# Rebuilding the setup of a one-core attention and mixture-of-experts block

## What is computed

```python
mod = (silu(c) @ wmod).reshape(8, 6, 1, -1)            # sa, ca, ga, sb, cb, gb
h = layernorm(x) * (1 + ca) + sa
c_q = h @ w_dq.T                                       # 256 -> 192
q_c, q_r = c_q @ w_uq.T, c_q @ w_qr.T                  # content 16 x 16, rotary 16 x 64
c_kv = h @ w_dkv.T                                     # 256 -> 64, "latent"
k_c, v, k_r = c_kv @ w_uk.T, c_kv @ w_uv.T, h @ w_kr.T
q_r, k_r = rope(q_r, k_r)
x = x + ga * (softmax(mask(q @ k.T) * SCALE) @ v @ w_out.T)
h = layernorm(x) * (1 + cb) + sb
x = x + gb * experts(h)     # top-8 router over 32, 8 merged groups, silu(gate) * up, down
```

## Time and profile before

| what | value |
|---|---|
| time of the timed runs | 1141.07 us median of 3, 1139.87 to 1143.53 |
| time of the profiled execution | 1138.69 us |
| its span, first to last instruction | 1136.6 us |
| mean granted TensorE clock | 0.977 |
| PE busy | 1031.2 us, 91% |
| DVE busy | 754.6 us, 66% |
| ACT, POOL busy | 399.5 us and 419.9 us, 35% and 37% |
| first `score` matmul of batch 0 | 95.21 us from the start |

### The profile page before, as it was taken

One profiled execution on the slowest core, in us unless ns is written; L12 is line 12 of the kernel. 1 busy time (PEld: TensorE's weight loads), 2 busy tenths in 40 slices (PEclk: granted clock), 3 DMA queues, 4 the chain that ended last, 5 costly groups with the idle time before them and its releaser, 6 DMA issues.

```text
span 1136.6 us, 24953 instructions
## 1 busy us (share of the span) xinstructions
PE 1031.2 (91%) x9856; PEld 743.4 (65%) x9856; DVE 754.6 (66%) x1516; ACT 399.5 (35%) x715; POOL 419.9 (37%) x349
## 2 busy tenths in 40 slices
PE   7849999999999998999999998999999999999668
PEld 2636667766677666766677666776677666776456
DVE  3557858677676767668676777668586776766335
ACT  1432542145331642244422553225421543315310
POOL 1152643164342632244332633326431633426100
PEclk9978999999999999999999999999999999999979
DMA  6130000010002000020002000020001100010000
GB/s 193 28 103 2 2 2 1 25 43 2 1 1 67 2 2 1 2 66 2 2 1 66 2 2 1 1 67 1 2 1 37 31 2 1 1 48 2 2 0 19
DMA packets 22152, 23.59 MB, mean 21 GB/s; under 512 B 6298, under 2 KB 20058, under 8 KB 22050
## 3 DMA queue, kind: packets, MB, share of 16 engines
q1 hardware_dynamic: 22050, 22.02, 6.4%
HBM read 17.80 MB, written 4.21 MB: 19 GB/s over the span
## 4 chain that ended last, share of the span: by engine, by line
PE 82%; DVE 8%; issue 4%; ACT 4%; POOL 1%; DMA 1%; DVEq 0%; SPq 0%; POOLq 0%; ACTq 0%
PE ring L1083 16%; PE ring L947 12%; PE ring L948 10%; PE ring L949 10%; PE ring L1152 7%; PE av L1099 6%; PE ring L1063 6%; DVE mcol L829 3%; PE ring L1054 3%; PE ring L1071 1%; PE ring L1143 1%; PE ring L1007 1%; PE av L1112 1%; ACT pt L648 1%; ACT xn L607 1%
## 5 line engine op out<-in xcount | busy, mean ns | idle before, releaser
L648 ACT ACTIVATE pt<-ring 128x384 f32<-128x384 f32 (+1 forms) x384 | 171.0, 532 | 361.9 <-PE ring L1083 319.3
L829 DVE TENSOR_REDUCE mcol<-ring 128x1 f32<-128x128 f32 (+3 forms) x512 | 212.0, 483 | 51.8 <-PE ring L1063 49.7
L544 POOL TENSOR_SCALAR_AFFINE_SELECT pt<-pt 128x512 f32<-128x512 f32 x128 | 83.3, 663 | 350.3 <-ACT pt L648 350.3
L805 DVE TENSOR_TENSOR prod<-ring,table 128x1024 f32<-128x1024 f32 x128 | 156.1, 1222 | 78.4 <-PE ring L949 56.7
L1083 PE MATMUL ring<-rows 32*128 32x512 f32 (+3 forms) x3072 | 164.4, 327 | 20.5 <-DVE mcol L829 10.5
L535 POOL TENSOR_TENSOR rows<-prod,rows 128x1024 fp32r<-128x1024 f32 x64 | 152.4, 2385 | 82.5 <-ACT rows L628 82.5
L1083 PEld LDWEIGHTS ring<-rows 32*128 32x128 f32 x3072 | 119.3, 184 | 68.9 <-issue 35.3
L528 POOL TENSOR_TENSOR prod<-prod 128x512 f32<-128x512 f32 x64 | 84.7, 1323 | 134.2 <-DVE prod L805 133.9
L947 PE MATMUL ring<-h_hi,gu_lo 128*128 128x512 f32 x192 | 80.3, 418 | 14.2 <-DVE h_lo L790 14.2
L1099 PE MATMUL av<-pt,vals 128*17 128x512 f32 (+3 forms) x1024 | 83.4, 439 | 10.2 <-POOL pt L544 10.2
L947 PE MATMUL ring<-h_hi,wq_lo 128*128 128x512 f32 x192 | 83.8, 436 | 3.8 <-DVE cont L817 3.3
(11 more groups left out here) (157 smaller groups left out, 1650.8 us busy)
## 6 DMA issues: line engine op xcount, KB each, us to landing
xn<-x_dram SPq DMA_DIRECT2D x8, 512.0 KB, 4.1
xr<-x_dram SPq DMA_DIRECT2D x8, 512.0 KB, 3.8
out_dram<-xr SPq DMA_DIRECT2D x8, 512.0 KB, 3.1
gate_bc<-gates_scratch SPq DMA_DIRECT2D x8, 256.0 KB, 5.2
pt<-wmod_dram SPq DMA_DIRECT2D x1, 1536.0 KB, 9.0
pt<-gup_t_dram SPq DMA_DIRECT2D x16, 96.0 KB, 2.5
prod<-wu_t_dram SPq DMA_DIRECT2D x1, 640.0 KB, 5.0
xr<-wk_t_dram SPq DMA_DIRECT2D x1, 512.0 KB, 8.8
```

Source lines behind the costliest of these rows:

```text
L648: sc.activation(pt[:, PT_AT[n] + h * w:PT_AT[n] + (h + 1) * w], ps[:, 0:w], ACT.Exp, scale=SCALE).then_inc(exp_ready.sem, 1)
L805: ve.tensor_tensor(prod[:, s % PROD, :, :], ps[:, :].unsqueeze(1).broadcast_to([P, 2, S]), table[:, :, :], ALU.mult).then_inc(rotated.sem, 1)
L829: last = ve.reduce_max(mcol[:, q, h * HR + HD:h * HR + HD + 1], ps[:, at:at + (q + 1) * P], AX_X)
```

## The change

Only the setup is different; the list of the last batch is now written out (`LAST_ORDER`), and it has the same 185 steps in the same order as the filtered list had.

- The loads are issued in another order: the index list, `c` and `wmod` first, then `x`, the latent weights, the keys' weights, the weights for fusing, the small ones and the tables. `wu` and `w_dq` no longer go to `prod`: they go to `dn`, `room` and `wo`, so the loads of `wo` and of the down weights wait on SP for `fuse_read` of all six pieces. The 16 loads of gate and up weights stay behind `gates_read`.
- The order of the steps is new: `silu`, the layer norm, `mod`, the splits of the latent and key weights, `turn1`, `gates`, `modulate1`/`low1`, `fuse` 0, the split of the other small weights, `latent`. `fuse` 1 stands before the first `rope`, `fuse` 2 and 3 (the content columns) before group 1, `fuse` 4 and 5 (columns of groups 2 and 3) before `qcon.01`.
- `split_keys` is three steps with a count each. DVE's part of `gates` now stands ahead of `low1`.
- `kcon_hi`/`kcon_lo` stand ahead of `hi` of the same group, and `maxima`/`reduce` of group 0 between the steps of group 1. `shift.00` comes after `qcon.01`, and `spread` and both `split_ffn` are last.

```diff
-FUSE = [(c, at, min(512, NQ - at)) for c in range(EC) for at in range(0, NQ, 512)]
+FUSE = [(c, at, min(512, NQ - at)) for at in (0, NG * NROPE, 512) for c in range(EC)]
-latent.0 latent_hi.0 latent_lo.0 rope.0000 rotate.0000 rope.0001 rotate.0001 combine.000 kcon.00 hi.000 kcon_hi.00
-kcon_lo.00 lo.000 rope.0010 rotate.0010 rope.0011 rotate.0011 combine.001 qcon.00 hi.001 qcon_hi.00 qcon_lo.00
-lo.001 values.00 values_out.00 values.01 values_out.01 rope.0100 rotate.0100 rope.0101 rotate.0101 combine.010
-kcon.01 hi.010 kcon_hi.01 kcon_lo.01 lo.010 rope.0110 rotate.0110 rope.0111 rotate.0111 combine.011 qcon.01 hi.011
-qcon_hi.01 qcon_lo.01 lo.011
+latent.0 latent_hi.0 latent_lo.0 fuse.1 rope.0000 rotate.0000 rope.0001 rotate.0001 combine.000 kcon.00 kcon_hi.00
+kcon_lo.00 rope.0010 rotate.0010 rope.0011 rotate.0011 hi.000 lo.000 combine.001 fuse.2 fuse.3 hi.001 lo.001
+rope.0100 rotate.0100 qcon.00 qcon_hi.00 qcon_lo.00 rope.0101 rotate.0101 combine.010 values.00 values_out.00
+values.01 values_out.01 kcon.01 kcon_hi.01 kcon_lo.01 hi.010 maxima.000 reduce.000 lo.010 rope.0110 rotate.0110
+maxima.001 reduce.001 rope.0111 rotate.0111 combine.011 maxima.002 reduce.002 fuse.4 fuse.5 qcon.01 qcon_hi.01
+qcon_lo.01 shift.00 shifted.00 hi.011 lo.011 spread. split_ffn.0 split_ffn.1
...
-    out = [("stats1", 0), ("pow1", 0), ("fuse", 0), ("norm1", 0)] + [("fuse", i) for i in range(1, len(FUSE))]
-    out += [("silu",), ("mod",), ("split_keys",), ("turn1", 0, 0), ("turn1", 0, 1), ("modulate1", 0, 0), ("low1", 0, 0),
-            ("modulate1", 0, 1), ("low1", 0, 1), ("gates",)]
-    out += steps_of(SETUP_ORDER) + [("spread",)]
-    for i in range(NMAX):
-        out += [("maxima", 0, 0, i), ("reduce", 0, 0, i)]
-    return out + [("split_ffn", 0), ("shift", 0, 0), ("shifted", 0, 0), ("split_ffn", 1)]
+    out = [("silu",), ("stats1", 0), ("pow1", 0), ("norm1", 0), ("mod",), ("split_d",), ("split_k",), ("turn1", 0, 0), ("turn1", 0, 1),
+           ("gates",), ("modulate1", 0, 0), ("low1", 0, 0), ("modulate1", 0, 1), ("low1", 0, 1), ("fuse", 0), ("split_uv",)]
+    return out + steps_of(SETUP_ORDER)
...
+            chosen_at = [sp.value_load(idx_sb[0:1, g:g + 1], min_val=0, max_val=NX - 1) for g in range(G)]
             for g in range(G):
...
+            sp.wait_ge(fuse_read, len(FUSE))
+            sp.dma_start(wo[:, :, :], wo_p.rearrange("g p e -> p g e")).then_inc(ld_wo, 16)
+            for g in range(G):
                 for row, n in DOWN_PIECES[g]:
...
                     elif kind == "rope":
-                            pe.wait_ge(fuse_read, len(FUSE))
+                            pe.wait_ge(fuse_read, EC)
...
                     elif kind == "qcon":
+                        if part == "setup":
+                            pe.wait_ge(fuse_read, len(FUSE) if g else 2 * EC)
...
                     elif kind == "down":
+                        if isinstance(b, int) and b == 0 and i == 0:
+                            pe.wait_ge(ld_down, 16 * sum(map(len, DOWN_PIECES)))
```

More of the change, by code:

```diff
@@ L116, in body_steps @@
-def body_steps(last):
-    return [s for s in steps_of(BODY_ORDER) if s[1] == 0 or not last]
+LAST_ORDER = """
+loads.0 maxima.010 reduce.010 rope.0200 score.000 rotate.0200 exp.000 rope.0201 rotate.0201 maxima.011 rope.0210
+reduce.011 score.001 clear.000 combine.020 rotate.0210 rope.0211 exp.001 clear.001 maxima.012 value.000 rotate.0211
+value.001 reduce.012 score.002 shift.01 exp.002 combine.021 kcon.02 qcon.02 clear.002 kcon_hi.02 hi.020 shifted.01
+score.010 lo.020 qcon_hi.02 value.002 exp.010 hi.021 kcon_lo.02 clear.010 qcon_lo.02 attn_out.00 rope.0300 score.011
@@ new lines @@
+exp.011 lo.021 rope.0301 rotate.0300 maxima.020 value.010 rotate.0301 reduce.020 score.012 rope.0310 exp.012
+maxima.021 rotate.0310 reduce.021 combine.030 clear.011 clear.012 rope.0311 kcon.03 maxima.022 rotate.0311 qcon.03
+hi.030 value.011 kcon_hi.03 lo.030 qcon_hi.03 combine.031 hi.031 kcon_lo.03 reduce.022 value.012 qcon_lo.03 shift.02
+shifted.02 maxima.030 reduce.030 attn_out.01 score.020 exp.020 lo.031 score.021 exp.021 clear.020 maxima.031
+reduce.031 maxima.032 value.020 clear.021 reduce.032 value.021 score.022 shift.03 shifted.03 exp.022 clear.022
@@ new lines @@
+score.030 value.022 exp.030 attn_out.02 score.031 clear.030 exp.031 score.032 value.030 exp.032 clear.031 value.031
+clear.032 value.032 attn_out.03 mix.00 mix.01 mixed.00 mixed.01 stats2.0 pow2.0 norm2.0 turn2.00 turn2.01
+modulate2.00 modulate2.01 low2.00 low2.01 up.00 gate.00 logits.0 tanh.00 gated.00 gate.01 logits_out.0 gate.02
+tanh.01 top.0 gated.01 up.01 ex.0 tanh.02 upped.00 gate.03 gate.04 top2.0 turn_w.0 up.02 gated.02 tanh.03 wT.0
+gated.03 gate.05 upped.01 upped.02 tanh.04 tanh.05 gated.04 wT_lo.0 up.03 up.04 weigh.00 upped.03 weigh.01 weigh.02
@@ L236, in block_program @@
         av = ctx.enter_context(nc.psum_tensor("av", [P, 512], F32))
[L239 to L240 removed]
+        ld_wo, ld_d, ld_mod, ld_q, ld_k, ld_tab, ld_small, ld_ffn, ld_down, ld_idx = (
+            sem(n) for n in ("ld_wo", "ld_d", "ld_mod", "ld_q", "ld_k", "ld_tab", "ld_small", "ld_ffn", "ld_down", "ld_idx"))
         x_loaded = Count(sem("x_loaded"), 1, 16)
@@ L426, in x_rows @@
                 return x[bass.ds(b + ahead, 1), :, :].rearrange("o (t p) e -> p (o t) e", p=P)
+            sp.dma_start(idx_sb[:, :], chosen).then_inc(ld_idx, 16)
+            sp.dma_start(ct[:, :, :], c_t.rearrange("(c p) b -> p c b", p=P)).then_inc(ld_mod, 16)
+            sp.dma_start(wmod_st, wmod.rearrange("(c p) n -> p c n", p=P)).then_inc(ld_mod, 16)
+            sp.dma_start(xn[:, :, :], x_rows(0, 0)).then_inc(x_loaded.sem, 16)
+            sp.dma_start(wd_st, wdkv_t.rearrange("(c p) n -> p c n", p=P)).then_inc(ld_d, 16)
+            for c in range(EC):
+                sp.dma_start(wk_st[c], wk_t[c * P:(c + 1) * P, :]).then_inc(ld_k, 16)
             sp.dma_start(wdq_st[:, 0, :], w_dq[0:P, :]).then_inc(ld_q, 16)
             sp.dma_start(wdq_st[0:CQ - P, 1, :], w_dq[P:CQ, :]).then_inc(ld_q, 16)
[L431 to L440, removed]
+            sp.dma_start(wu_main, wu_t[0:P, :]).then_inc(ld_q, 16)
+            sp.dma_start(wu_rest, wu_t[P:CQ, 0:NG * NROPE]).then_inc(ld_q, 16)
+            sp.dma_start(wu_rest_con, wu_t[P:CQ, NG * NROPE:NQ]).then_inc(ld_q, 16)
             for copy in range(2):
@@ L469, in _ @@
             sp.wait_ge(gates_stored, 16)
-            sp.wait_ge(keys_split, 1)
+            sp.wait_ge(keys_split, 2 + EC)
             def program(sp, b, part, steps):
@@ L1010, in program @@
                         if part == "setup":
-                            pe.wait_ge(keys_split, 1)
+                            pe.wait_ge(keys_split, 1 + EC)
                         ps = take_bank(pe, b, part, step)
@@ L1035, in program @@
                         i = step[2]
+                        if part == "setup":
+                            pe.wait_ge(keys_split, 2 + EC)
                         ps = take_bank(pe, b, part, step, [(latent_ready, ahead, 0)])
```

61 lines of the change are left out of this document (37 added, 24 removed).

## The result

The changed kernel takes 1120.12 us (median of 4 runs, 1117.11 to 1122.87) against 1140.47 us for the kernel before in the same comparison: a ratio of 0.982, with a 95% interval from 0.9802 to 0.9837, and 20.4 us less by the medians. The profiled execution took 1118.26 us, also 20.4 us less than the one before.

The account below looks back on a forecast made before the run. Batches were taken as bound by PE, the first 95 us by a chain of waits; `reduce.010` 20.5 us earlier, less 1.5 us of hand-overs, gains 19: 1141.07 - 19 = 1122 us, own range 1119 to 1124, 8-in-10 range 1115 to 1130.

Parts of the forecast that it names:

- the 73 to 77 given as a sign: End of the setup: `reduce.010` on DVE was to start at 73 to 77 us in the new profile, against 93.87 before.
- PE fast from early on: Rival for the setup: all fuse pieces and `mod` at half price, gain 22 to 26 us; chance 0.14.
- Part 1: Setup up to the first projection: `wmod` lands at 9.3, the latent starts at 26.5 instead of 44.9, 18.4 us earlier.
- The early fuse pieces: Setup on PE: `fuse` 0 hidden from 22.4 to 26.4, `fuse` 1 at 4.0 us ahead of the first `rope`.
- The pace of the combinations: The four combinations on POOL: 6.0 us pace instead of about 7.6; starts at 36.5, 42.5, 48.8 and 57.9.
- `fuse` 2 and 3 hide; `fuse` 4 and 5 do not: Setup on PE: `fuse` 2 and 3 (2.3 us each) hide beside POOL; `fuse` 4 and 5 cost 5.8 us at the end.
- The maxima "beside the ropes": Group 0's maxima and reductions, in the setup: what was serial from 81.70 to 89.9 us now lies beside the ropes.
- The end: Last setup steps, `fuse` 4 to `reduce.010`: `qcon.01` 1.4 us, `spread` 1.65, `split_ffn` low parts 3.4; `reduce.010` at 73.4 before hand-overs.
- The clock's slices: Profile page before the change: the granted clock was read as low only in the third and fourth slices.
- SP's queue: Loads moved past SP: `x` of batch 1 issued at 75 to 78, landed by 83, needed at 92; costs nothing, 9 us spare.
- The rival of the late `x`: Batch 1: `x` issued behind `fuse_read` and thirteen loads lands too late, kernel slower than before at 1147 us; chance 0.02.

## Why the prediction was right

The forecast was 1122 us with a gain of 19; the gain is 20.4. The sign, the place of the gain (the setup alone) and most of the path were right. That the size agrees so well is luck. At the point that the sum was worked out for, the start of `reduce.010`, the gain is 24.9 us and not 19: it came at 69.00, outside the 73 to 77 given as a sign. There the rival "PE fast from early on" (22 to 26) is nearer, although `mod` kept its full price. Behind that point about 4.4 us were lost which the sum did not have: 0.2 up to the first score, 2.2 to the clock by the layer norm of batch 1, and 2.1 later, most of it in the tail.

- **Part 1.** `wmod` landed at 8.1 (6.44 us), not 9.3, and `silu` took 0.7 for 0.9: `mod` began at 8.83, not 10.2. From there the steps have their rows' prices (7.00, 1.80, 3.42, then DVE's gates 21.07 to 24.34), and the latent begins at 25.08 for 26.5. Right, with the landing 1.2 us oversized.
- **The early fuse pieces.** They were costed at 4.0 us because every piece of 512 columns in the trace had taken that. This step failed: they took 2.1 from the first one on. It was the term that the rival "PE fast from early on" had right for the fuse pieces and wrong for `mod`. With `fuse` 1 cheap (`fuse` 0 was hidden either way) and the latent 1.4 us sooner, the first combination is at 32.97 for 36.5.
- **The pace of the combinations.** 6.0 forecast, 6.06 measured. Right, and the run with `hi` first shows the cause. The fourth came at 53.29 for 57.9, behind the reductions as forecast.
- **`fuse` 2 and 3 hide; `fuse` 4 and 5 do not.** Right. 4.3 us for 5.8.
- **The maxima "beside the ropes".** The step said that what was serial now lies beside them, as a gain. The run with the maxima late shows no gain from the place: the first score comes 2.2 us sooner without it, of which 1.7 are `spread`. The serial stretch itself is hardly shorter there (55.12 to 62.96, 7.8 us, for 8.3 before), but `qcon.01` comes 6.9 us sooner (51.48 for 58.35), which is most of what it costs. I did not ask what the reductions hold up on DVE.
- **The end.** `qcon.01` took 2.95 us (granted clock 0.51 there) for 1.4, `spread` 2.29 for 1.65. Together 2.2 us that I had not counted. `reduce.010` at 69.00 for 73.4 plus hand-overs.
- **What I took as given:** that the first score follows at the same price as before. It cost 1.7 us more at a granted clock of 0.50, after 4.54 us of idling, and the projection behind it 0.5 more. So 24.7 us at the score became 22.5 in the batches.
- **The clock's slices.** I read them as low only in the third and fourth. The last but one reads 7 too; it is in that tail that 2.0 us were lost, and it is not in the sum.
- **SP's queue.** `x` of batch 1 was issued at 68.33 and was no one's wait. The rival of the late `x` did not come up.

The runs also say what single parts are worth, at the first score: the new head 8.5 us, of which PE's pace is the mechanism; the content copies ahead of `hi` 7.7; the pieces 0; the maxima beside group 1, with `spread` beside POOL, minus 2.2. One of them was taken against the kernel before and three against the changed one, so they need not add up to 24.7. What is left (10.7) no run separated. Of it 5.7 us would be `mod` starting at 8.83 and not at 14.51 as in the run with the modulation first, for which the load order is needed; the cause of the other 5.0 stays open.

## What to carry to other kernels

In a setup, ask which of its steps runs PE at which pace, from the duration of like instructions in two places, before costing it from its own row: the same matmuls cost 20.7 us or 11.2 us, by what PE did before them. Work that is moved beside other work gains only if its engine was idle there and nothing behind it in that engine's order is in the chain; here the reductions held up the rotations. Where DVE and POOL work side by side, ask also which POOL instruction lies beside each DVE instruction: `spread` cost 0.61 or 2.36 us by that alone. And a change of a few instructions ahead of a loop can move a halt at the turn of the loop into the open, worth more than the edit itself, so read the loop's first step again after every change of the code ahead of it.

## What the runs showed of the hardware that I had not expected

- Long fp32 fusing from the start of the program never got faster in 20 us (1.0 us for a matmul of 512 columns), but the same matmuls ran at 0.53 us behind `mod`, `turn1` and `gates`, and stayed so for 11 us. In all these stretches the granted clock reads 1.00. It read 1.00 until its first fall (about 46 us before, behind 55 us in the changed kernel), at either pace; up to there only the durations of like matmuls tell the levels apart.
- Behind the latent the clock fell in two profiles of nearly the same program (granted clock 0.50 from 28 to 32 us, first combination at 35.75 and 35.79) and not in four others (1.00; 32.97, 32.98, 32.84 and 32.73). PE had idled 2.35 and 2.31 us ahead of the latent in the two, and 1.94, 1.86, 2.26 and 2.06 us in the four. The longer idle times are those before the fall, but six profiles are too few to say that they are its cause. `fuse` 1 took 3.9 us in one of the two, for 1.9 in the changed kernel:

```profile
26.23 1.91 PE L1026 MATMUL ring<-dn,wo 128*128 128x512 f32 x2
28.07 2.07 PE L1028 MATMUL ring<-room,wo 64*128 64x512 f32 x2
```

- After the turn of the loop PE halts for 0.5 to 1.8 us at a place fixed in its instruction stream (10, 14 and 19 matmuls into the loop with 14, 10 and 5 matmuls added ahead of it). Behind it, with 14 and 10 added, the clock fell too, and a batch was 2.4 and 2.0 us longer on the mean. The changed kernel without added matmuls shows no such halt within a step.
- A DVE `tensor_scalar` from SBUF to SBUF (`spread`) took 0.61 us alone and up to 2.83 us beside a POOL instruction, ending 0.4 us after it each time. In the run with the maxima late it came first (54.58), and there POOL's low part took 2.64 us for 2.4 elsewhere.
